# Attention scores of a four-layer graph network: three fp32r products on the full array, or plain fp32 products on its two 64-row halves

## What is computed

```python
q = (x @ Wq + bq).reshape(b, n, H, HD)      # H, HD = (8, 64)
k = (x @ Wk + bk).reshape(b, n, H, HD)
v = (x @ Wv + bv).reshape(b, n, H, HD)
scores = jnp.einsum('bihd,bjhd->bhij', q, k) / jnp.sqrt(jnp.float32(HD))
scores = scores + jnp.where(adj == 0, -1e9, 0.0)[None, None, :, :]
weights = jax.nn.softmax(scores, axis=-1)
out = jnp.einsum('bhij,bjhd->bihd', weights, v)
```

## Time and profile before

| | |
|---|---|
| median of 3 executions | 2856.92 us (2856.85 to 2857.3) |
| the profiled execution | 2855.93 us, of which the span is 2854.1 us |
| PE busy | 2773.0 us, 97% of the span |
| PEld / DVE / ACT / POOL busy | 2514.3 / 2151.3 / 1631.1 / 1507.2 us |
| mean granted TensorE clock | 0.990 of full speed |
| matmul records | 18569 |

### The profile page before, as it was taken

One profiled execution on the slowest core, in us unless ns is written; L12 is line 12 of the kernel. 1 busy time (PEld: TensorE's weight loads), 2 busy tenths in 40 slices (PEclk: granted clock), 3 DMA queues, 4 the chain that ended last, 5 costly groups with the idle time before them and its releaser, 6 DMA issues.

```text
span 2854.1 us, 59257 instructions
## 1 busy us (share of the span) xinstructions
PE 2773.0 (97%) x18569; PEld 2514.3 (88%) x18569; DVE 2151.3 (75%) x6805; ACT 1631.1 (57%) x4616; POOL 1507.2 (53%) x1808
## 2 busy tenths in 40 slices
PE   4899999999999999999999999999999999999996
PEld 3799998999999999999999999899999999999986
DVE  7777777777777777777777777777777777777763
ACT  3455656655555556556555555655555555556553
POOL 6555555545545555555555555555555555555541
PEclk9999999999999999999999999999999999999997
DMA  3000000000000000000000000000000000000000
GB/s 119 16 20 27 30 18 26 29 18 26 28 20 26 26 22 26 26 22 26 26 22 26 26 22 26 20 27 26 18 26 29 18 26 29 18 26 29 9 16 23
DMA packets 41471, 74.06 MB, mean 26 GB/s; under 512 B 5584, under 2 KB 5712, under 8 KB 41424
## 3 DMA queue, kind: packets, MB, share of 16 engines
q1 hardware_dynamic: 41424, 73.49, 7.9%
HBM read 39.92 MB, written 33.55 MB: 26 GB/s over the span
## 4 chain that ended last, share of the span: by engine, by line
PE 96%; DVE 1%; issue 1%; ACT 1%; DMA 0%; POOL 0%; ACTq 0%; SPq 0%; POOLq 0%; DVEq 0%
PE rot L812 22%; PE rot L814 22%; PE rot L813 22%; PE rot L912 9%; PE rot L920 4%; PE rot L869 4%; PE score L812 2%; PE score L813 2%; PE score L814 2%; PE rot L961 2%; PE rot L889 2%; PE rot L893 2%; PE att_bank L942 0%; PE s_bank L877 0%; DMA probs<-in_L_gnn_W 0%
## 5 line engine op out<-in xcount | busy, mean ns | idle before, releaser
L337 POOL TENSOR_TENSOR ve<-mv,eps_col 128x1 f32<-128x1 f32 (+1 forms) x448 | 95.2, 212 | 679.6 <-DVE mv L609 351.2
L359 POOL TENSOR_TENSOR x2b<-x,bias 128x512 f32<-128x512 f32 x128 | 216.4, 1690 | 448.5 <-DVE x L657 448.5
L812 PE MATMUL rot<-w_hi,y_hi 128*128 128x512 f32 x1024 | 426.5, 417 | 5.4 <-DVE y_lo L649 4.6
L814 PE MATMUL rot<-w_hi,y_lo 128*128 128x512 f32 x1024 | 404.4, 395 | 0.0
L813 PE MATMUL rot<-w_lo,y_hi 128*128 128x512 f32 x1024 | 402.8, 393 | 0.0
L437 ACT ACTIVATE k_hi<-rot,kb_col 64x256 fp32r<-64x256 f32 x512 | 240.5, 470 | 271.6 <-PE rot L814 266.7
L551 ACT ACTIVATE probs<-score,sc_nmax 128x128 f32<-128x128 f32 x1024 | 357.8, 371 | 11.4 <-DVE sc_nmax L773 11.4
L599 DVE SCALAR_TENSOR_TENSOR k_lo<-rot,kb_col,k_hi 64x256 fp32r<-64x256 f32 x512 | 247.5, 483 | 93.3 <-ACT k_hi L437 87.7
L912 PEld LDWEIGHTS rot<-v_sb,probs_t 128*128 128x128 f32 x2048 | 241.5, 194 | 69.8 <-issue 58.5
L812 PE MATMUL rot<-xt_hi,wk_hi 128*128 128x256 f32 x1024 | 299.8, 293 | 0.0
L599 DVE SCALAR_TENSOR_TENSOR q_lo<-rot,qb_col,q_hi 128x256 fp32r<-128x256 f32 x256 | 112.1, 479 | 239.9 <-ACT q_hi L437 239.9
(11 more groups left out here) (122 smaller groups left out, 8383.2 us busy)
## 6 DMA issues: line engine op xcount, KB each, us to landing
x_in<-in_x SPq DMA_DIRECT2D x128, 256.0 KB, 2.6
out_x<-x SPq DMA_DIRECT2D x128, 256.0 KB, 2.1
probs<-in_L_gnn_W SPq DMA_DIRECT2D x1, 1024.0 KB, 7.6
v_sb<-in_L_gnn_weight SPq DMA_DIRECT2D x1, 1024.0 KB, 7.1
probs<-in_L_gnn_Wv SPq DMA_DIRECT2D x1, 1024.0 KB, 5.5
v_sb<-in_L_gnn_Wq SPq DMA_DIRECT2D x1, 1024.0 KB, 5.4
probs<-in_L_gnn_Wk SPq DMA_DIRECT2D x1, 1024.0 KB, 5.1
x<-in_L_gnn_a SPq DMA_DIRECT2D x1, 512.0 KB, 4.6
```

Source lines behind the costliest of these rows:

```text
L359: pool.tensor_tensor(x2b[:, :], x2[:, slot.buf(L_GCN, 2), :], bias2[:, :], ALU.add)\
L812: pe.matmul(outp, lh, rh, start=first, stop=False)
L814: return pe.matmul(outp, ll, rh, start=False, stop=last)
```

## The change

Queries and keys are kept once, in plain fp32 (`q_sb`, `k_sb`), with their bias added by ACT. No low parts are made, and the two DVE steps that made them are gone. The keys have no zeroed slots, so ACT copies them in two 128x256 instructions and not in four 64x256 ones. The scores are eight plain fp32 matmuls of 64 rows by 128 columns, one for each block, graph and head: head 0 on partitions 0 to 63 into score bank 0, head 1 on partitions 64 to 127 into bank 1. The DVE and ACT loops over the score tiles go head by head, since a bank now holds one head. Two small moves go with it: DVE's `aggregate("3")` stands behind `y1_lo`, and the memsets of `k_hi` and `k_lo` at the start are gone.

```diff
-        q_hi, q_lo = (sb(f"q_{n}", [P, CHUNKS, GROUP * P], F32R) for n in ("hi", "lo"))
-        k_hi, k_lo = (sb(f"k_{n}", [P, CHUNKS, GROUP, 2, P], F32R) for n in ("hi", "lo"))
+        q_sb = sb("q_sb", [P, CHUNKS, GROUP * P])
+        k_sb = sb("k_sb", [P, CHUNKS, GROUP * P])
...
+        def score_tile(c, g, h):
+            return score_bank[h][:, (c * GROUP + g) * P:(c * GROUP + g + 1) * P]
...
-            for k in (k_hi, k_lo):
-                pool.memset(k[:, :, :, :, :].bitcast(F32), 0.0).then_inc(k_zero, 1)
...
-                        for h, rows in enumerate(HEAD_ROWS):
-                            ins = biased(k_hi[rows, c, :, h, :], k_bank(c, rows), kb_col[rows, chunk:chunk + 1])
-                    ins.then_inc(k_hi_done, 1)
+                        ins = biased(k_sb[:, c, :], k_bank(c), kb_col[:, chunk:chunk + 1])
+                    ins.then_inc(k_done, 1)
...
-                    for c in range(CHUNKS):
-                        chunk = slot.part(L_QK) * CHUNKS + c
-                        ins = biased_low(q_lo[:, c, :], q_bank(c), qb_col[:, chunk:chunk + 1], q_hi[:, c, :])
-                    ins.then_inc(q_lo_done, 1)
...
-                            ins = biased_low(k_lo[rows, c, :, h, :], k_bank(c, rows), kb_col[rows, chunk:chunk + 1],
-                                             k_hi[rows, c, :, h, :])
-                    ins.then_inc(k_lo_done, 1)
...
-                    slot.wait(pe, q_lo_done, L_QK)
-                    slot.wait(pe, k_lo_done, L_QK)
+                    slot.wait(pe, q_done, L_QK)
+                    slot.wait(pe, k_done, L_QK)
...
-                            ins = three(score_bank[c][:, g * 2 * P:(g + 1) * 2 * P],
-                                        [a[:, c, g * P:(g + 1) * P] for a in (q_hi, q_lo)],
-                                        [b[:, c, g, :, :].rearrange("p h n -> p (h n)") for b in (k_hi, k_lo)],
-                                        True, True)
+                            cols = slice(g * P, (g + 1) * P)
+                            for h, rows in enumerate(HEAD_ROWS):
+                                ins = pe.matmul(score_tile(c, g, h), q_sb[rows, c, cols], k_sb[rows, c, cols],
+                                                start=True, stop=True)
```

More of the change, by code:

```diff
@@ L597, in _ @@
                .then_inc(consts_done, 1)
-            def biased_low(dst, src, bias, high):
-                return dve.scalar_tensor_tensor(out=dst, in0=src, scalar=bias, in1=high.bitcast(F32),
-                                                op0=ALU.add, op1=ALU.subtract)
             def statistics(n, src, g=0):
@@ L637, in emit @@
                     slot.wait(dve, st_done["3"], L_OUT)
-                if slot.on(L_QK):
-                    slot.wait(dve, q_hi_done, L_QK)
-                    for c in range(CHUNKS):
-                        chunk = slot.part(L_QK) * CHUNKS + c
-                        ins = biased_low(q_lo[:, c, :], q_bank(c), qb_col[:, chunk:chunk + 1], q_hi[:, c, :])
-                    ins.then_inc(q_lo_done, 1)
-                if last:
-                    aggregate("3", 0, GROUP)
                 if slot.on(L_GAT):
@@ L650, in emit @@
                         .then_inc(y1_lo_done, 1)
+                if last:
+                    aggregate("3", 0, GROUP)
                 if slot.on(L_GCN):
@@ L694, in emit @@
                     aggregate("0", slot.buf(L_EDGE, 2))
-                if slot.on(L_QK):
-                    slot.wait(dve, k_hi_done, L_QK)
-                    for c in range(CHUNKS):
-                        chunk = slot.part(L_QK) * CHUNKS + c
-                        for h, rows in enumerate(HEAD_ROWS):
-                            ins = biased_low(k_lo[rows, c, :, h, :], k_bank(c, rows), kb_col[rows, chunk:chunk + 1],
-                                             k_hi[rows, c, :, h, :])
-                    ins.then_inc(k_lo_done, 1)
                 if slot.on(L_ATT):
@@ L768, in emit @@
                 if slot.on(L_QK):
-                    for c in range(CHUNKS):
-                        for t in range(TILES):
-                            tile = score_bank[c][:, t * P:(t + 1) * P]
-                            ins = dve.tensor_tensor_reduce(out=tile, in0=tile, in1=mask[:, :], scale=-SCALE,
-                                                           scalar=3.0e38, op0=ALU.add, op1=ALU.min,
-                                                           accum_out=sc_nmax[:, c, t:t + 1])
+                    for h in range(2):
+                        for c in range(CHUNKS):
+                            for g in range(GROUP):
+                                tile, t = score_tile(c, g, h), g * 2 + h
+                                ins = dve.tensor_tensor_reduce(out=tile, in0=tile, in1=mask[:, :], scale=-SCALE,
+                                                               scalar=3.0e38, op0=ALU.add, op1=ALU.min,
+                                                               accum_out=sc_nmax[:, c, t:t + 1])
                         ins.then_inc(score_nmax_done, 1)
@@ L890, in emit @@
                     ins.then_inc(pt0_mm, 1)
-                    slot.wait_last(pe, (q_lo_done, L_QK, 0), (pt1_done, L_PV, 1))
+                    slot.wait_last(pe, (q_done, L_QK, 0), (pt1_done, L_PV, 1))
                     for t in range(TILES):
```

44 lines of the change are left out of this document (22 added, 22 removed).

## The result

The changed kernel takes **2788.85 us** (median of 4 executions, 2788.56 to 2791.56) against 2856.89 for the kernel before in the same session, a ratio of 0.9764 with a 95% interval of 0.9747 to 0.9781. It is 68 us faster; 2788 was forecast. The terms of that sum were less exact than the sum: two were too small, one too large, and they cancel, so that the last microsecond of agreement is luck. The profiled execution was the longest of the four, 2791.56 us, so what is read from the trace adds up to 64 us and not 68.

A forecast was written before the change was run, and what follows sets the result against it. PE, busy 97% of the span, was taken as the bound. Gap −30, draining slots −4, score overlap −55 and row switches +20 sum to −69 us: 2788 us median, 8-in-10 range 2762 to 2882 us.

The forecast's parts named there:

- PE is the bound, and DVE's work is worth nothing: PE is busy 97% of the span; dropping the low parts of q and k from DVE gains nothing.
- The gap at L912 is ACT's queue: Weights-times-values product on PE waits for ACT's second probs_t copy; a shorter key copy closes the gap, −30 us.
- The scores on PE: Eight plain fp32 score matmuls replace a 1.44 us block: −55 us with overlap, +20 us for row switches.
- overlap: Score matmuls on the two array halves run side by side: 1.01 us a block, −0.43 a slot, −55 us.
- the ninth step: Score matmuls start in program order, so overlapped halves take 8 + 1 steps of 0.1125 us.
- step between 128 and 64 rows: Switching rows twice a slot around the scores costs nothing to 41 us; half, 20 us, was taken.
- The draining slots: In four draining slots PE waits outright for ACT at L912; the shorter key copy takes 1.08 us off each, −4 us.
- What is late next: x3 transposes after the scores wait for y2_lo; slack 0.65 us, overlap takes 0.43, so it does not bind.
- The signs: Expected profile readings: key copy 0.84 us, slot 20.9 to 21.0, draining wait 1.25, L912's "issue" row gone.
- No overlap: Rival: weight loads of both halves go one after the other, score block 1.80 us, 2869 to 2910 us; chance 0.27.
- Partial overlap: Rival: only every other load of the other half hides, score block 13 distances, 1.46 us, 2846 us; chance 0.10.
- The gap did not stay: Rival that the gap at L912 stays, held by the step to plain fp32 or something unseen: 2818 us; chance 0.06.

The follow-up runs named there:

- The run with the copies first: Changed kernel with ACT's two copies of the transposed weights put ahead of the attention's exponential; 2783.40 us, ratio 0.9744 to the kernel before.
- the gap alone: Kernel before, scores untouched, with ACT's two copies of the transposed weights put ahead of the attention's exponential; 2817.93 us.
- the run on all rows: Changed kernel with each score matmul over all 128 rows, so each tile holds the sum of both heads; 2858.28 us.

## Why the prediction held, point by point

*PE is the bound, and DVE's work is worth nothing.* Right in the steady slots: with the keys' part of DVE's work put back they take the same time, and the medians differ by 2.5 us with ranges that overlap.

*The gap at L912 is ACT's queue.* Right, and shown twice: closing it alone by another edit gave −38 us, opening it again in the changed kernel took 43.5 with the draining slots. **The size was short.** The sum had (0.23 + 0.27)/2 × 122 = −30 and left out that a released matmul also runs its first weight load in the open, 0.07 us. Of the 38 us on offer the changed kernel has taken some 33, because `att_nmax` from DVE still comes late: L486 waits for it 118 us in 128 slots, where it was 30 us in 5. The forecast had a margin of 0.35 us here. It was smaller, since the loads can start with the forerunner (1506.92 and not 1507.05, as its own shows), and the forecast took it that `att_nmax` comes no later. It does, in every second slot:

```profile
ACT att_p L486 <- DVE att_nmax L677: 118.2, 128, 7.4
...
1494.97 1.44 POOL L359 TENSOR_TENSOR x2b<-x,bias 128x512 f32<-128x512 f32 x1 [3.19 <-DVE x L643]
1495.19 1.37 DVE L658 SCALAR_TENSOR_TENSOR att_e<-z 128x128 f32<-128x128 f32 x1
...
1516.60 0.28 DVE L658 SCALAR_TENSOR_TENSOR att_e<-z 128x128 f32<-128x128 f32 x1
```

L658 is an earlier step of the same chain on DVE. It took 1.37 us in 62 of the 128 slots of the changed kernel and 0.28 in the other steady ones; in the kernel before the same step took 1.37 us twice, while the pipeline filled. Each time POOL's L359 is at work beside it, but so it is where L658 is short. Why the same instruction takes five times as long was not tried and stays open. In the late slots ACT's exponential waits 1.0 us for `att_nmax` and not 0.5, and the copies behind it miss the forerunner by about 0.1 us. The run with the copies first fetched the rest.

*The scores on PE.* The forecast was −55 + 20 = −35 us. Measured, by rows: from L942 at 1510.82 to the product with `w2` at 1512.71 before, 1.89 us; from L920 at 1502.94 to L790 at 1504.65 now, 1.71; −0.18 × 128 = **−23 us**, and the run with four key copies leaves 24. The term was mis-sized in two parts that go against each other. The *overlap* was better than its bound: 8 pairs and not 9 steps, 0.90 us and not 1.01, because the first records of both halves start together. The claim that matmuls start in program order, on which the ninth step rested, is false across halves. The *step between 128 and 64 rows* was taken at half of its bound, 0.08 us a time; it is 0.17, the whole of it, 44 us in place of 20. The forecast named more than 0.16 us for each switch as a sign that it is wrong, and by that sign it is, by 0.01. By the Trainium skill, "TensorEngine Tiling (Array Packing)", Key Properties, tiles load weights and multiply in parallel and a change of tiling mode drains the engine; the trace agrees with the first, with 0.112 us for a pair, the distance of one. With the second it agrees in that starts stand 0.20 us apart and not 0.11 at either change; that the array is empty in between it does not show.

*The draining slots.* −4 us forecast, −10 measured in the drain. L912's wait was 1.2 us shorter in each of four (2.33 to 1.12 us in the one shown), 5 us, and the scores of the slots in the drain give about 1. What else the drain gave has a row too, for the window from 2794 to 2800 of the kernel before and from 2736 to 2742 of the changed one (busy time by engine, then the granted clock):

```profile
2794.00:2800.00 6.00, 6.00 (x30) 6.00 (x30) 1.42 (x4) 1.12 (x2) 1.95 (x2) 0.50 0.24 90
...
2736.00:2742.00 6.00, 5.39 (x45) 4.90 (x46) 2.98 (x18) 3.57 (x12) 2.53 (x2) 1.00 0.23 87
```

Before, PE had waited 2.3 us at L912 in the slots just ahead, and the clock was granted at half, 1.2 GHz: the score matmuls there stand 0.21 us apart and not 0.12. With the shorter waits it stayed at 2.4 GHz there and fell in a later slot only, and for a shorter time. The less time at half the clock is worth at most 3 to 4 us, half of the 7 us by which it shrank. No run tried this by itself, but the other traces fit. Leaving out the last fall, which lasts to the end, the half clock lasted 10 to 17 us of the drain in the three runs with waits of 2.3 us at this product (the kernel before, the gap alone, the key copy in four) and 0 to 7 us in the ten with shorter ones. It varies that much among kernels with the same waits, so a few microseconds of the drain are chance.

*What is late next.* Right: y2_lo did not bind here, and did in the two runs that made the block ahead of it shorter. The slack came out near the forecast's 0.22 us, again by two errors: it left out the 0.15 us from y2_lo's end to the start that it releases, and the block shrank by 0.25 us and not by 0.43. Left are 1504.24 − 1503.82 − 0.15 = 0.27 us.

*The sum.* Forecast −30 − 4 − 35 = −69 us. By the runs some −33, −10 and −23, which is −66, between the 64 us of the two profiled executions and the 68 of the medians. The terms are off by 3, 6 and 12 us with opposite signs; that the median came out within 1 us is luck, that it came out far from the rivals is not.

*The signs.* The key copy reads 0.84 us and the slot 21.07, against 20.9 to 21.0 expected. PE's wait in the draining slots reads 1.12 us, against 1.25. The "issue" row is not gone but down from 58.5 us to 13.9. From the first score to the follower of the x3 transposes it is 1.51 us (1503.14 to 1504.65), outside both the 1.0 to 1.3 for overlap and the 1.8 for none; the sign fits only up to L940, 1.10 us, and left out the transposes.

*The rivals.* No overlap is refuted by the pairs. It would have given +12 us, and the run on all rows, which is that rival without the steps, came out at +2. Partial overlap occurs only if the order of the heads is changed: with four of each in a row the block takes the 13 distances of that rival. The gap did not stay.

## What to carry to other kernels

A wait that the profile puts down to "issue" is worth a look at the instruction's semaphores: here it hid the engine whose queue was full, and saving two instructions there gave more than the new arithmetic did. Two half-height matmuls cost as much as one, loads included, if they alternate between the halves. Against that stand 0.34 us for each change to 64 rows and back. In plain fp32 a matmul on alternating halves saves 0.112 us as compared with all rows, so that by this estimate four of them more than earn the change back. A block that shrinks uncovers what ran beside it, so look up the next release before counting on the whole gain.

## What the runs showed of the hardware that was not expected

- The other half's next record may start some four records ahead of its turn: with four matmuls of a head in a row, 16 records took 13 distances of 0.11 us, alternating 8, in twos 9. Which half a record is on is worked out from the starts.
- A change from 128 rows to 64 and back costs 0.34 us, 0.17 each way. That is about what a matmul's drawn length is above its distance (0.28 − 0.12). Twice as many changes cost twice as much.
- A matmul released late by a semaphore loses, besides the wait, 0.07 us of its block, because the first weight load no longer runs beside the work ahead.
- One DVE instruction on the same operands took 0.28 us in some slots and 1.37 in others, beside the same POOL instruction. The cause is open.
- Writing both heads' tiles into one bank at the same time was not tried.
